# One step sequence over six layers, feed-forward groups inside it; exponentials without accumulator, row sums on VectorE

## The reference

```
for i in range(DEPTH):                       # DEPTH = 6
    x = attn_layer(shift_tokens(x), Wqkv[i], q_scale[i], k_scale[i], Wo[i]) + x
    x = ffn_layer(shift_tokens(x), ln_g[i], ln_b[i], W1[i], b1[i], W2[i], b2[i]) + x

def attn_layer(x, Wqkv, qs, ksc, Wo):        # 16 heads of 64, windows of 32 tokens
    q, k, v = split(x @ Wqkv)
    q = rotary(l2norm(q) * qs); k = rotary(l2norm(k) * ksc)
    return local_attention(q, k, v) @ Wo     # each window sees itself and the one before

def ffn_layer(x, g, bln, W1, b1, W2, b2):    # inner size 341
    xn = (x - mu) / sqrt(var + 1e-05) * g + bln
    a, gate = split(xn @ W1 + b1)
    return a * gelu(gate) @ W2 + b2
```

## Time and profile before

| what | value |
|---|---|
| median of 3 runs | 3575.65 us (3574.94 to 3576.36) |
| the profiled execution | 3575.57 us, its span 3573.7 us |
| busy share of the span | PE 91%, PEld 62%, DVE 78%, ACT 82%, POOL 57% |
| mean granted TensorE clock | 0.958 of 2.4 GHz |
| bytes by DMA | 57.58 MB, mean 16 GB/s |

### The profile page before, as it was taken

How to read it: one execution, slowest core, us unless ns; L and a number is a source line. 1 busy time by engine, 2 the same in 40 slices (tenths; PEclk the granted TensorE clock), 3 DMA queues, 4 the chain that set the end, 5 groups by cost and what they waited for, 6 DMA issues and landing times. The chain is left out here.

```text
span 3573.7 us, 118257 instructions
## 1 busy us (share of the span) xinstructions
PE 3252.6 (91%) x42076; PEld 2208.0 (62%) x42076; DVE 2791.6 (78%) x5370; ACT 2933.6 (82%) x9257; POOL 2045.7 (57%) x2150
## 2 busy tenths in 40 slices
PE   5699998889999789999789999978999977999977
PEld 4466665656666556666566666665666655666656
DVE  7788887578888568888658888757888856888865
ACT  3399998479999459999649999937999955999973
POOL 3566665456666356666446666545666634666644
PEclk8799999899999899999899999989999989999999
DMA  2000001100000100000110000010000010000011
GB/s 70 10 7 8 7 7 33 22 13 7 7 7 6 47 15 8 7 7 7 37 24 7 8 7 7 10 44 14 7 8 7 6 43 19 8 7 7 7 34 42
DMA packets 141061, 57.58 MB, mean 16 GB/s; under 512 B 118598, under 2 KB 137668, under 8 KB 139460
## 3 DMA queue, kind: packets, MB, share of 16 engines
q1 hardware_dynamic: 140484, 50.01, 5.9%
HBM read 22.57 MB, written 2.10 MB: 7 GB/s over the span
## 5 line engine op out<-in xcount | busy, mean ns | idle before, releaser
L1321 ACT ACTIVATE probs<-s_ps,nbias,rnorm 128x64 f32<-128x64 f32 x3072 | 1229.9, 447 | 1.6 <-DVE nbias L1039 0.9
L1524 POOL TENSOR_TENSOR qk_rot<-by_cos,by_sin 128x1024 f32<-128x1024 f32 x384 | 914.0, 2380 | 381.9 <-DVE by_sin L989 334.8
L597 PE MATMUL ring<-wvo,xsT 128*32 128x512 f32 x6144 | 794.8, 600 | 10.2 <-ACT vo L1144 10.2
L1321 ACT ACTIVATION_READ_ACCUMULATOR probs<-s_ps,nbias,rnorm 128x1 f32 x3072 | 765.0, 249 | 0.0
L1513 POOL TENSOR_TENSOR probs<-probs,rrow 128x256 f32<-128x256 f32 x768 | 454.6, 613 | 429.1 <-DVE rrow L973 429.1
L986 DVE TENSOR_TENSOR by_cos<-qk_ps,rotary 128x1024 f32<-128x1024 f32 x378 | 463.0, 1225 | 147.1 <-ACT squares L1307 147.1
L1533 POOL TENSOR_TENSOR qk_rot<-qk_rot,rnorm 128x1024 f32<-128x1024 f32 x192 | 365.5, 1904 | 341.4 <-DVE rnorm L733 341.4
L543 PEld LDWEIGHTS ring<-cst,qk_rot 128*128 128x128 f32 x3072 | 341.3, 141 | 243.7 <-ACT vo L1144 155.9
L543 PE MATMUL ring<-cst,qk_rot 128*128 128x128 f32 x3072 | 446.4, 278 | 27.6 <-POOL qk_rot L1524 24.4
L1001 DVE TENSOR_REDUCE sumsq<-squares 128x16 f32<-128x1024 f32 x384 | 462.9, 1206 | 0.0
L989 DVE TENSOR_TENSOR by_sin<-qk_ps,rotary 128x1024 f32<-128x1024 f32 x378 | 459.2, 1215 | 0.0
(11 more groups left out here) (166 smaller groups left out, 5433.4 us busy)
## 6 DMA issues: line engine op xcount, KB each, us to landing
qk_rot<-L_ffn_Wqkv SPq DMA_DIRECT2D x7, 1024.0 KB, 5.1
xs<-x_tok SPq DMA_DIRECT2D x194, 32.0 KB
xs<-x_tok SPq DMA_DIRECT2D x194, 31.8 KB
by_cos<-x_tok SPq DMA_DIRECT2D x48, 128.0 KB
by_cos<-x_tok SPq DMA_DIRECT2D x48, 127.0 KB
wv<-L_ffn_Wqkv SPq DMA_DIRECT2D x7, 512.0 KB, 6.6
wo_pad<-L_ffn_Wo SPq DMA_DIRECT2D x14, 256.0 KB, 7.3
xs<-x_tok SPq DMA_DIRECT2D x194, 0.2 KB
```

Source lines behind the costliest of these rows:

```text
L597: last = mm(r[WIN * mh:WIN * (mh + 1), :], xsT[:, a, WIN * w:WIN * (w + 1)], wvo[:, mh, :, :], start=True, stop=True)
L1321: last = nc.scalar.activation(probs[:, a, h // 4, :, h % 4, :], s_ps[:, half, c:c + 2 * WIN].rearrange("p (s c) -> p s c", s=2), ACT.Exp, ...
L1524: g.tensor_tensor(qk_rot[:, n, :], by_cos[:, n, :], by_sin[:, n, :], ALU.add).then_inc(added[qk], 1)
```

## The change

The loop over layers goes. `every_step(step)` writes out `STEPS` = 201 steps for the 192 tiles of all layers (`TILES`), with layer l's tile 0 right behind layer l-1's tile 31. A step keeps the stagger (tile k projected, k-3 put out), and a group of four tiles goes through the feed-forward part inside the steps: `group(k, f)` is the group whose part f falls into step k, or None. Counting k modulo 4: in steps of kind 3 `centre`, its squares (now on POOL), the deviation, POOL's inverse deviation, and for an older group `down` and `x_new`; in kind 0 `normalised`, its transposes, three `gate` products and `up` 0; in kind 1 `gelu`, `up` 1, `hidden` 0; in kind 2 `hidden` 1, `up` 2, `hidden` 2. All of them use the four banks of `ring` (`ring_uses`, counted through), no longer qk_ps and s_ps. Weights of the next layer are loaded and prepared during the steps (`next_values`, `next_wqk_upper`, `next_table`), into space of their own (`wide`, `w1_hi`, `w1_lo`). ln_g is folded into w1 and ln_b into b1 (`bias_product`, six matmuls of one column a layer). The output is written group by group in the last layer.

In the attention part: `accum_out` goes; DVE sums the rows (`row_sums`, one reduction of 512 a half); the half-kT and the vo copy that DVE had go to ACT; `rotate("k")` and `square("k")` move into the step after; the order of all calls is new.

```diff
+            return (here(GROUPS, ("b1", layer_at(k, 7)))
+                    + here(TILES, ("qT0", k - 1), ("pT0", k - 3))
+                    + here(GROUPS, ("up2", group(k, 4)), ("xn", group(k, 2)))
+                    + here(TILES, ("xsT", k), ("pT1", k - 3), ("vo3", k - 2), ("o", k - 3), ("vo1", k - 1))
+                    + here(GROUPS, ("gate0", group(k, 2)), ("gate1", group(k, 2)), ("gate2", group(k, 2)))
+                    + here(TILES, ("qT1", k - 1))
+                    + here(GROUPS, ("down", group(k, 5)), ("up0", group(k, 2)), ("up1", group(k, 3)))
...
 # PE
+                probs_transposed(1, 3)
+                project("q", 0, 0)
+                project("q", 1, 0)
+                values(3, 2)
+                output(3)
+                values(1, 1)
+                up("gate", 0, group(k, 2))
+                up("gate", 1, group(k, 2))
+                up("gate", 2, group(k, 2))
+                transposed("q", 1, 1)
+                down(group(k, 5))
+                up("up", 0, group(k, 2))
+                up("up", 1, group(k, 3))
+                project("k", 0, 0)
+                project("k", 1, 0)
...
 # DVE
+                    dve.wait_ge(exp_done[half], done(T))
+                    p = probs[:, a, 2 * half:2 * half + 2].rearrange("p q s h c -> p q h s c")
+                    v.tensor_reduce(psum_row[:, h].rearrange("p (q h) -> p q h", q=2), p, AXY,
+                                    ALU.add).then_inc(row_summed[half], 1)
...
 # ACT
-                                scale=rnorm[:, a, h:h + 1], bias=nbias[:, h:h + 1],
-                                accum_out=psum_row[:, h:h + 1])
+                            scale=rnorm[:, a, h:h + 1], bias=nbias[:, h:h + 1])
...
+                exponentials(0, 2)
+                square("q", 0)
+                next_wqk_upper(next_layer_at(k, NT - 1 + 0), 0)
+                exponentials(1, 2)
+                xsT_evacuated(0)
+                exponentials(2, 2)
+                exponentials(3, 2)
+                vo_evacuated(3, 2)
+                vo_evacuated(1, 1)
...
 # POOL
+                    g.tensor_tensor(xn4[:, :, :], xs4[:, :, :], xs4[:, :, :], ALU.mult).then_inc(norm_g["squared"], 1)
```

More of the change, by code:

```diff
@@ L31 @@
 AX = mybir.AxisListType.X
+AXY = mybir.AxisListType.XY
 P = 128
@@ L89, in constants @@
     first[0:WIN, 0:WIN] = NEG
[L90 to L91 removed]
+    parts["mask"] = np.concatenate([first, mask], 1)
     h = np.arange(P) // D0
@@ L316, in schedule, with every_step, there @@
                 step(k, k % 2, None)
-        def every_tile(step, depth, before_last=None):
-            for k in range(NT + depth):
-                if before_last and k == NT + depth - 1:
-                    before_last()
+        def every_step(step):
+            for k in range(STEPS):
                 step(k)
-        def tile_numbers(l, k):
-            return k, NT * l + k
-        def there(k, it, s, n=NT):
+        def there(k, it, s, n=TILES):
             return it is not None or 0 <= k - s < n
@@ L347, in passed @@
             return n + CREDIT
-        def ahead(engine, value):
-            engine.compute_val(value)
-            return value
         @block.tensor
@@ L676, in down @@
+                def down(U):
+                    if U is None:
+                        return
+                    r = bank_of("down", U)
+                    pe.wait_ge(w2_in, 32 * (U // NG) + 32)
+                    pe.wait_ge(g_hid, passed(3 * U + 3))
+                    for t in range(FT):
                         for i in range(3):
-                            block = hid[:, i, :] if i else hid_first[par]
-                            last = mm(ring[:, 1, t * C:(t + 1) * C], block[:, t * P:(t + 1) * P], w2[:, i, :],
+                            last = mm(r[:, t * C:(t + 1) * C], hid[:, i, t * P:(t + 1) * P], w2[:, i, :],
@@ L710, in _, with bias_product @@
-                down(NG - 1, 1, FT // 2, FT)
-                for r in range(2, WVO_ROUNDS):
-                    wvo_product(r, l + 1)
+                    last.then_inc(g_down, 1)
+                def bias_product(l):
+                    if l is None:
+                        return
+                    r = bank_of("b1", l)
+                    pe.wait_ge(w1_in, 16 * l + 16)
+                    pe.wait_ge(ln_in, 32 * l + 32)
+                    for j in range(2):
+                        for i in range(3):
+                            c = j * F + FB[i][0]
+                            last = mm(r[:, 3 * j + i:3 * j + i + 1], w1[:, c:c + P], ln_col[:, 1:2],
+                                      start=True, stop=True)
+                    last.then_inc(b1_ps, 1)
@@ L1135, in _, with biases @@
-            dve.wait_ge(x_ready, NT * (DEPTH + 1))
-            for b in range(B):
-                tiles = x_keep[:, b * TPB:(b + 1) * TPB, :]
-                v.tensor_tensor(tiles, tiles, x_cols(b * TPB, TPB), ALU.add).then_inc(final_ready, 1)
+                def biases(l):
+                    if l is None:
+                        return
+                    dve.wait_ge(b1_in, 96 * l + 96)
+                    dve.wait_ge(b1_ps, l + 1)
+                    v.tensor_tensor(b1_col[:, :], ring[:, ring_bank["b1", l], 0:6], b1_raw[:, :],
+                                    ALU.add).then_inc(b1_ready, 1)
@@ new lines, in step @@
+                rotate("k", 0, 1)
+                rotate("k", 1, 1)
+                sum_of_squares("k", 1)
+                maxima(0, 2)
+                hidden(2, group(k, 4))
+                centre(group(k, 1))
+                xsT_lower(0)
+                lower(group(k, 2))
+                inverse_norms(0, 1, 1)
+                softmax_bias(0, 2)
+                inverse_norms(1, 2, 1)
+                maxima(1, 2)
+                inverse_norms(2, 3, 1)
+                softmax_bias(1, 2)
@@ L1141, in _ @@
+                inverse_norms(3, 8, 1)
+                group_deviation(group(k, 1))
+                rotate("q", 0, 0)
+                rotate("q", 1, 0)
+                residual(3)
+                row_sums(0, 2)
+                row_sums(1, 2)
+                x_new(group(k, 5))
+                sum_of_squares("q", 0)
+                row_reciprocals(0, 2)
+                row_reciprocals(1, 2)
+                w1_lower(layer_at(k, 7))
+            every_step(step)
         @block.scalar
@@ L1227, in step @@
                     for half in range(2):
-                        wvT_evacuated(half, 0)
+                        wvT_evacuated(half, 0, ring[:, 0, :])
             def first_wqk_upper(k):
@@ L1491, in first_weights @@
                 pool.wait_ge(rotary_in, 16)
-                tables(0)
+                pool.wait_ge(sc_in, 32)
+                for j in range(TPB):
+                    table(0, j).then_inc(tables_ready, 1)
                 for part in range(2):
```

1449 lines of the change are left out of this document (708 added, 741 removed).

## The result

| | before | changed |
|---|---|---|
| median | 3575.3 us (3574.53 to 3576.36, 4 runs) | 3704.9 us (3700.36 to 3706.43, 4 runs) |
| ratio to before | 1 | 1.036, 95% interval 1.0342 to 1.0378 |
| span of the profiled execution | 3573.7 us | 3703.5 us |
| mean granted TensorE clock | 0.958 | 0.979 |

A forecast was written before the change was run, and what follows sets the result against it. PE was taken as the bound, busy 91%, with only idle time to win. 263.7 + 3179 (46 cycles of 69.1) + 40 + 21 + 29 + 1.9 = 3535 us, range 3400 to 3655.

The forecast's parts named there:

- to step 8: Front unchanged, tile 0's residual at 193.7 us, then 5 steps of 14.0 without groups, to 263.7 us.
- 46 ordinary cycles: Steps 8 to 192: 46 cycles of four steps, 69.1 us each with stalls of 6.5, together 3179 us.
- seams and next weights: Weights of five next layers: transposes, products, copies and bias columns, 8 us each, 40 us.
- from step 192 on: Last two steps 21 us, last group's way from residual to output 29, beside the span 1.9.
- PE's own work: Four steps of 13.7 us without small waits, plus 7.8 for a group: 62.6 us a cycle.
- The waits for the ring: PE waits for ring banks ACT frees late, 1.5 us each in kinds 0, 1 and 3: 4.5 a cycle.
- The lateness: ACT's first exponentials late after pq: 1.2 us in kind 1, 0.5 in kind 3, 0.3 in kinds 0 and 2 together.
- The seams: Rival: next layer's first tile waits for projections' weights or tables, 10 to 20 us at five seams; chance 0.04.
- The slower rival: Kind 3 late through POOL's squares holding DVE and late tokens; cycle 70.2 to 71.7 us, 3585 to 3654; chance 0.30.
- The break-even: The old time, 3575.65 us, is met at a cycle of 70.0 us, with stalls of 7.4.
- The signs that I named: Residuals 17.3 us apart on average, about 19, 17, 15, 18.5 by kind; ACT busy near 90%; clock at 1.00.
- The other rivals: Exponential 0.16 us and PE the bound, 3236 to 3346, chance 0.12; table loads with drain, 3653, chance 0.05.

The follow-up runs named there:

- best2: Changed kernel with seam calls moved, group work behind the k projection, ACT copies earlier, squares on ACT and exp table loaded early: 3400.9 us, ratio 0.952.
- vo3_early: Changed kernel with ACT's copy of v3 put one group of exponentials earlier: 3603.9 us, ratio 1.0086.
- relu: Changed kernel with Relu in the place of Gelu, so no table is loaded in the steps: 3599.1 us, ratio 1.0072.
- behind_pk: Changed kernel with PE's down, up 0 and up 1 moved behind the two halves of the k projection: 3612.1 us, ratio 1.0112.
- before_late: Kernel before with the copies of v3 and v1 moved behind exponentials(12) and (14): 3839.9 us, ratio 1.0737.
- seam: Changed kernel with DVE's biases moved behind maxima(0) and SP's next-layer loads behind the group's tokens: 3654.5 us, ratio 1.0226.
- squares_act: Changed kernel with the centred group's squares on ACT instead of POOL, and its variance ahead of the inverse norms' third step: 3699.9 us, ratio 1.0351.

## Why the prediction was wrong, step by step

The forecast was 170 us too low. By the residual's times, tile 5 at 280.4 and tile 189 at 3643.7 us, four parts make it up:

| part | forecast | measured | off by |
|---|---|---|---|
| to step 8 | 263.7 | 280.4 | 17 |
| 46 ordinary cycles | 46 x 69.1 = 3179 | 46 x 71.5 = 3289 | 110 |
| seams and next weights | 40 | 3363.3 - 3289 = 74 | 34 |
| from step 192 on | 52 | 61 | 9 |

My cycle was too short, which turned a small gain into a loss. It didn't carry the time out of the range: 71.5 lies below the 71.7 at the range's upper end, and 355.6 + 46 x 71.5 is 3645. The other three lines, 60 us in terms that had no range, did.

To split the cycle I measure as the forecast does, from start to start, and call waiting what a pair of pieces takes beyond its usual distance where nothing holds it up (in `best2`, if not in the changed kernel itself; at `up` and `down` behind tq1 I take the 0.41 of the k projection in kind 2):

| place | start to start | without a wait | wait | forecast |
|---|---|---|---|---|
| kind 0, first to second gate, last matmul to first | 1.30 | 0.23 | 1.07 | |
| kind 0, tq1 to `up` 0 | 1.00 | 0.41 | 0.59 | both 1.5 |
| kind 1, tq1 to `up` 1 | 1.86 | 0.41 | 1.45 | 1.5 |
| kind 3, tq1 to `down` | 1.86 | 0.41 | 1.45 | 1.5 |
| kind 1, out to v1 | 3.41 | 1.75 | 1.66 | 1.2 |
| kind 3, pT1 to its q projection | 1.04 | 0.41 | 0.63 | |
| kind 3, out to v1 | 2.16 | 1.75 | 0.41 | both 0.5 |
| kinds 0 and 2, out to v1 | 1.98 each | 1.75 | 0.46 | 0.3 |

That is 7.7 us; with pieces under 0.1 it is 7.8 in this cycle and 7.4 in the next. What is left, 71.8 - 7.8 and 71.2 - 7.4, is 64.0 and 63.9, and `best2` gives 63.9 too. So of the 2.4 us by which the cycle was short, 1.3 are work of PE and 1.1 are waits.

**PE's own work: the first step that failed.** I put four steps with a group at 62.6 us; they take 63.9, 60 us over 46 cycles. The base was 13.7 us for a step "without such small waits". I had read the value windows of 0.95 to 0.97 us, where 0.88 was possible, as windows that waited. What follows sets them: ahead of the output a window takes 0.88, ahead of transposes 0.97 with no wait (1045.41 to 1046.38 in `best2`). The stretch from kind 2's v3 to the next, which holds no piece of a group, takes 15.0 us in `best2`, 1.0 of it waiting: 14.0, as before. So 14.01 was the number to take, and 4 x 0.3 are nearly all of the 1.3. The group's pieces, 7.8 by the forecast, take 7.9.

**The waits for the ring: right in size, place and cause.** Forecast 4.5 us, measured 4.6. What I named first, the exponential at 0.29 us, was 0.29. `vo3_early`, `relu`, `behind_pk` and `before_late` confirm the mechanism from four sides.

**The lateness: right in place, too small.** Forecast 2.0 us, measured 3.2 in this cycle and 2.8 in the next, some 45 us over the run. In kind 1 xsT comes 1.66 late where I had 1.2. In kind 3 `centre` costs 0.63 at the q projection, and v1 waits 0.41 more. Kinds 0 and 2 have 0.46.

**The seams: the right rival with the wrong place.** I asked for a wait on `wq_ready` or `tables_ready` and gave it 0.04. The traces show neither. The 50 us of `seam` come from `biases`, which stood at the head of DVE's step in the diff, and from nine loads ahead of a group's tokens in SP's queue. I had counted the bias columns among eight microseconds of small work and not asked what is queued behind them. The first of the six waits for `biases` lies before step 8, so it stands in the table's first line. There, too, the residual of tile 0 runs at 200.1 us and not at 193.7: the front, which I had called unchanged, was 6 us later. Its cause stays open, as does that of the 9 us at the end.

**The slower rival: right sign, wrong mechanism.** It said that kind 3 comes late through POOL's lock and through tokens. The lock occurs, 1.00 us, and is worth 5 us in all (`squares_act`). Tokens are late five times, at seams, not 46. Its cycle, 70.2 to 71.7 us, did hold the measured one, by luck: by PE's base and by lateness in all kinds. The break-even was at waits of only 0.9 us above mine.

**The signs that I named.** The distances of residuals are 17.2, 20.4, 17.3 and 17.0 us for kinds 0 to 3 (medians, by the step that ends each), not "19, 17, 15, 18.5"; from v3 to v3 they are 19.0, 18.7, 15.0 and 19.1 or 18.7. ACT's mean share is 78% and not near 90%, which my own sum, 14 us in 17.3, had not given either.

**The other rivals.** The exponential isn't 0.16, and PE isn't the bound in the changed kernel; in `best2` it nearly is, with 63.9 of 65.7 us. A table load costs 1.1 us here, with no drain seen.

**What the parts of the change are worth.** The exponentials without accumulator: a gain of 365 us in the new kernel, some 130 of it the clock's, and a loss of 32 in the old one, where PE hardly waited for ACT. Copies on ACT: a gain of 41 us for the two tried. The single pipeline with this order: a loss, by waits of 7.6 us a cycle (350 us), of which `best2` leaves about 1.9, and by the seams (50).

## What to carry to other kernels

When a stage is folded into a pipeline, the idle time that vanishes comes back as waits at each shared buffer that is freed late: for each buffer, add up what its freeing engine does between the last thing it waits for and the copy, and put copies that free a bank ahead of work that nobody waits for. Take the measured step of an engine that is never idle as it stands: a piece that is longer than its shortest is a wait only if the same pair of pieces is closer together elsewhere. The test works both ways: 14.01 us here was work, while v1's 0.23 us of waiting shows in no idle time. Give each term a range, those outside the main loop too. At a seam, look at each operation that stands first in an engine's queue, however short, and at each load ahead of the next stage's data.
